# Attention probabilities split in SBUF and transposed by DMA instead of on TensorE

## The reference

```python
q = (x @ Wq).reshape(B, N, HEADS, DIM_HEAD).transpose(0, 2, 1, 3)   # 128 x 16 heads x 32 x 64
k = (context @ Wk).reshape(...)                                     # context: 257 rows of 96 for each sequence
v = (context @ Wv).reshape(...)
attn = softmax(einsum('bhnd,bhmd->bhnm', q, k) * SCALE)
out = einsum('bhnm,bhmd->bhnd', attn, v)
return out.transpose(0, 2, 1, 3).reshape(B, N, HEADS * DIM_HEAD) @ Wo + bo
```

## Time and profile before

| | before |
|---|---|
| median of the runs shown | 1027.83 us (1026.02 to 1030.45, 3 runs) |
| the profiled execution, its time | 1028.92 us |
| its span in the profile | 1027.0 us |
| TensorE busy | 870.6 us, 85% |
| VectorE busy | 831.1 us, 81% |
| GpSimd busy | 774.3 us, 75% |
| ScalarE busy | 684.0 us, 67% |

### The profile page before, as it was taken

One profiled execution on the slowest core, in us unless ns is written; L12 is line 12 of the kernel. 1 busy time (PEld: TensorE's weight loads), 2 busy tenths in 40 slices (PEclk: granted clock), 3 DMA queues, 4 the chain that ended last, 5 costly groups with the idle time before them and its releaser, 6 DMA issues.

```text
span 1027.0 us, 29818 instructions
## 1 busy us (share of the span) xinstructions
PE 870.6 (85%) x8554; PEld 720.6 (70%) x8554; DVE 831.1 (81%) x2343; ACT 684.0 (67%) x2029; POOL 774.3 (75%) x1237
## 2 busy tenths in 40 slices
PE   7989998999999999999999999999998461049895
PEld 7777786878787887878787887887776261036664
DVE  5899888989999989899999999998988657025563
ACT  3777776778777778778777777777775113037774
POOL 5788888898989898888889898989886503735554
PEclk9999999999999999999999999999999655559998
DMA  9111111111111111111111211111100840111120
GB/s 233 33 33 33 32 33 33 33 33 36 49 42 32 31 31 31 31 31 31 31 31 32 59 33 31 31 31 31 31 2 2 129 162 14 52 43 53 47 54 17
DMA packets 56836, 45.11 MB, mean 44 GB/s; under 512 B 8367, under 2 KB 54578, under 8 KB 56769
## 3 DMA queue, kind: packets, MB, share of 16 engines
q1 hardware_dynamic: 54464, 40.01, 15.9%
q0 software_dynamic: 2304, 4.25, 1.3%
HBM read 37.25 MB, written 7.52 MB: 44 GB/s over the span
## 4 chain that ended last, share of the span: by engine, by line
PE 36%; POOL 31%; issue 13%; DVE 12%; ACT 4%; DMA 1%; POOLq 1%; DVEq 1%; ACTq 0%; SPq 0%
POOL Pn L925 10%; PE bank L396 6%; PE bank L373 6%; PE bank L420 4%; POOL cT L916 4%; PE bank L1369 3%; PE bank L413 3%; PE bank L385 3%; POOL sorted_rows L1232 3%; POOL chi L906 2%; PE bank L1384 2%; DVE cs L839 2%; DVE nmax L783 2%; POOL clo L910 2%; DVE Tl L777 1%
## 5 line engine op out<-in xcount | busy, mean ns | idle before, releaser
L925 POOL TENSOR_TENSOR Pn<-Pe,rsum 128x1028 f32<-128x1028 f32 x128 | 243.1, 1899 | 74.4 <-DVE rsum L798 74.4
L713 ACT ACTIVATE Pe<-bank,nmax 128x257 f32<-128x257 f32 x512 | 240.5, 475 | 30.1 <-DVE nmax L783 29.5
L783 DVE TENSOR_REDUCE nmax<-bank 128x1 f32<-128x257 f32 x512 | 202.0, 415 | 35.3 <-PE bank L373 34.0
L373 PE MATMUL bank<-cT,qh 96*128 96x257 f16 x1024 | 184.8, 275 | 21.1 <-ACT Pe L713 19.6
L777 DVE TENSOR_TENSOR Tl<-bank,Th 128x512 f16<-128x512 f32 x256 | 173.8, 680 | 0.5 <-ACT Th L702 0.4
L702 ACT ACTIVATE Th<-bank 128x512 f16<-128x512 f32 x256 | 141.3, 595 | 48.5 <-PE bank L420 48.5
L420 PE MATMUL bank<-identf,Pn 128*128 128x128 f32 x1024 | 149.3, 274 | 0.0
L373 PE MATMUL bank<-cT,ql 96*128 96x257 f16 x512 | 139.2, 272 | 0.0
L420 PEld LDWEIGHTS bank<-identf,Pn 128*128 128x128 f32 x1024 | 115.1, 142 | 6.1
L373 PEld LDWEIGHTS bank<-cT,qh 96*128 96x128 f16 x1024 | 90.3, 97 | 38.3 <-issue 15.9
L713 ACT ACTIVATION_READ_ACCUMULATOR Pe<-bank,nmax 128x1 f32 x512 | 103.8, 203 | 0.0
(11 more groups left out here) (213 smaller groups left out, 2444.4 us busy)
## 6 DMA issues: line engine op xcount, KB each, us to landing
rawT<-in_dram SPq DMA_DIRECT2D x32, 385.5 KB, 3.9
raw<-in_dram SPq DMA_DIRECT2D x32, 384.0 KB, 4.4
sorted_rows<-fill SPq DMA_DIRECT2D x1, 2620.0 KB, 21.1
xs<-sorted_rows SPq DMA_DIRECT2D x40, 65.5 KB, 1.8
R<-in_dram SPq DMA_DIRECT2D x4, 512.0 KB, 5.9
Z<-last_rows SPq DMA_DIRECT2D x128, 2.2 KB
w1r<-in_dram SPq DMA_DIRECT2D x4, 512.0 KB, 13.7
w2fr<-in_dram SPq DMA_DIRECT2D x4, 512.0 KB, 14.2
```

What stands on the lines that cost most here:

```text
L373: last = nc.tensor.matmul(bank[SB[t]][:, 0:M], w[:, par, b, t * P:(t + 1) * P], cT[:, s4, c, 0:M], start=(k == 0), stop=(k == 2))
L713: nc.scalar.activation(Pe[:, n_par(j + 1), t, :], bank[SB[t]][:, 0:M], ACT.Exp, bias=nmax[:, n_par(j + 1), t:t + 1], accum_out=sums[:, n_p ...
L783: nc.vector.tensor_reduce(nmax[:, n_par(j + 1), t:t + 1], bank[SB[t]][:, 0:M], AX.X, ALU.max, negate=True).then_inc(s_nmax, 1)
L925: nc.gpsimd.tensor_tensor(Pn[:, par, :, :], Pe[:, par, :, :], rsum[:, par, :].unsqueeze(2).broadcast_to([P, QT, M]), ALU.mult)\
```

## The change

The probabilities are no longer transposed before they are split. ScalarE writes the high halves of Pn itself and VectorE the low halves, both into one SBUF tensor PHL, in two pieces h of two tiles each. A piece is 128 x 1024 f16, laid out as high or low (2), tile (2), column (256). SP then issues one crossbar DMA transpose for each piece into PT, which TensorE reads in `pe_pv`. The transposes of L420 are gone, as are Th and Tl. SP now follows the same steps as the other engines, and its context and Z loads stand between the transposes.

```diff
@@ pe_pv
-        def pe_pv(n, par, s8, gp, b, pairs):
+        def pe_pv(n, par, s8, gp, b, pairs, turns):
             wait(nc.tensor, s_Ol, n)
             k = 0
-            for w, p, s in ((chi, Th, s_Th), (clo, Th, None), (chi, Tl, s_Tl)):
+            for h in range(2):
+                wait(nc.tensor, s_T[par][h], 16 * turns)
+            for w, hl in ((chi, 0), (clo, 0), (chi, 1)):
                 for c in range(MC):
-                    if s is not None:
-                        wait(nc.tensor, s, MC * n + c + 1)
-                    nc.tensor.matmul(bank[6][0:CC, :], w[:, s8, c, :], p[:, par, c, :], start=(k == 0), stop=False)
+                    p = PT[:, par, :, :, :].rearrange("p h (l t c) r -> p h l t c r", l=2, t=2)
+                    nc.tensor.matmul(bank[6][0:CC, :], w[:, s8, c, :], p[:, :, hl, :, c, :], start=(k == 0), stop=False)
                     k += 1
@@ pe_step
-                wait(nc.tensor, s_pn, n + 1)
-                pe_probsT(n, n_par(j), 0)
             pe_mix(it, j, n)
             pe_early(n)
-            if exists(n):
-                pe_probsT(n, n_par(j), 1)
@@ act_step
-            if exists(n - 1):
-                wait(nc.scalar, s_PV, n - 2)
-                for c in range(MC):
-                    wait(nc.scalar, s_T, MC * (n - 1) + c + 1)
-                    nc.scalar.activation(Th[:, n_par(j - 1), c, :], bank[4 + c][:, :], ACT.Copy).then_inc(s_Th, 1)
+            if exists(n):
+                for h in range(2):
+                    wait(nc.scalar, s_T[n_par(j)][h], 16 * (4 * it + j // 2))
+                wait(nc.scalar, s_pn, n + 1)
+                for h in range(2):
+                    nc.scalar.activation(PHL[:, n_par(j), h, 0, :, :], Pn[:, n_par(j), 2 * h:2 * h + 2, 0:MC * P], ACT.Copy)\
+                        .then_inc(s_Ph, 1)
@@ dve_step
-                if kind == "low" and exists(n - 1):
-                    wait(nc.vector, s_Th, MC * (n - 1) + t + 1)
-                    nc.vector.tensor_tensor(Tl[:, n_par(j - 1), t, :], bank[4 + t][:, :], Th[:, n_par(j - 1), t, :],
-                                            ALU.subtract).then_inc(s_Tl, 1)
+                if kind == "low" and exists(n):
+                    wait(nc.vector, s_Ph, 2 * n + t + 1)
+                    nc.vector.tensor_tensor(PHL[:, n_par(j), t, 1, :, :], Pn[:, n_par(j), 2 * t:2 * t + 2, 0:MC * P],
+                                            PHL[:, n_par(j), t, 0, :, :], ALU.subtract).then_inc(s_Pl, 1)
@@ pool_step
-                wait(nc.gpsimd, s_T, MC * n)
+                wait(nc.gpsimd, s_Pl, 2 * n)
@@ SP
-            with sp.Fori(1, G // 2) as i:
-                for par in range(NP2):
-                    load_ctx(2 * i + par, par)
-                    load_z(2 * i + par, par)
+            def sp_step(it, j):
+                n, g, jj, gp = where(it, j)
+                if exists(n):
+                    wait(sp, s_PV, n - 1)
+                    for h in range(2):
+                        wait(sp, s_Pl, 2 * n + h + 1)
+                        sp.sem_inc(s_go)
+                        sp.dma_start(PT[:, n_par(j), h, :, :], PHL[:, n_par(j), h, :, :, :], transpose=True)\
+                            .then_inc(s_T[n_par(j)][h], 16)
+                if jj == 0 and exists(g + 2, G) and (n_static(n) is None or g >= 0):
+                    load_ctx(g + 2, gp)
+                if jj == 1 and exists(g + 1, G) and (n_static(n) is None or g >= 1):
+                    load_z(g + 1, 1 - gp)
+            pipeline(sp, sp_step)
```

More of the change, by code:

```diff
@@ L202, in perceiver_layer_kernel @@
         s_L12 = sem("s_L12")
-        s_T = sem("s_T")
-        s_Th = sem("s_Th")
-        s_Tl = sem("s_Tl")
+        s_T = [[sem(f"s_T{par}{h}") for h in range(2)] for par in range(NP2)]
+        s_go = sem("s_go")
+        s_Ph = sem("s_Ph")
+        s_Pl = sem("s_Pl")
         s_PV = sem("s_PV")
@@ L273, in perceiver_layer_kernel @@
         e12p = asb("e12p", [P, NP2, P], F16)
-        Th = asb("Th", [P, NP2, MC, Q], F16)
-        Tl = asb("Tl", [P, NP2, MC, Q], F16)
+        PHL = asb("PHL", [P, NP2, 2, 2, 2, MC * P], F16)
+        PT = asb("PT", [P, NP2, 2, 2 * 2 * MC, P], F16)
         L12 = asb("L12", [P, NP2, P], F16)
@@ L415, in pe_y @@
             last.then_inc(s_y, 1)
[L417 to L422, removed]
         def n_static(n):
@@ L442, in pe_step @@
                 pe_pv(n - 1, (j - 1) % NP2, (j - 1) % NC8, ((j - 1) // GB) % NP2, (j - 1) % GB,
-                      it + 1 + (j - 1) // NC8)
+                      it + 1 + (j - 1) // NC8, 4 * it + (j - 1) // 2 + 1)
             if exists(n - 5):
```

## The result

The changed kernel takes 1187.15 us in the median (1184.99 to 1192.66), the kernel before on the same chip 1026.92 (1025.72 to 1030.45): a ratio of 1.156, interval 1.151 to 1.161. It is 160 us slower. The profiled execution took 1186.75 us.

The account below looks back on a forecast made before the run. TensorE and VectorE lay close to the trip's length, GpSimd fixing some intervals; the change adds a ring and port waits. Steady trips 625, first four 232, last intervals 45: 902 against 759.5, +142, so 1170 us; own range 1128 to 1200.

Parts of the forecast that it names:

- the ring: Loop: Pn, its split, next exponentials, reciprocal of their sums, next Pn; one pass, 6.14 us, bounds every step from below.
- the port: VectorE instructions with two SBUF inputs and GpSimd's lock each other out; trip 56.8 us, or 54.0 if they never wait.
- TensorE's relief: Eight f32 transposes a step leave TensorE, 0.88 us a step, 7.0 a trip; priced at nothing.
- Rival 2: Loop: TensorE was the pace and ScalarE never waits for Pn; faster, 981 us; chance 0.05.
- the sum: Whole attention loop: eleven steady trips 625, first four 232, last seven intervals 45, together 902 us against 759.5.
- my loop without the port: Attention loop if subtractions never meet GpSimd: trips of 54.0 us, 858 us in all, execution 1128.
- The two SBUF inputs: Low-half subtractions beside GpSimd's chi, clo, cT: VectorE 0.2 us late, GpSimd 0.8, paid in its two full intervals.
- The single intervals: Eight step intervals of a steady trip, from j = -1 to 0 onward, each priced; together 56.8 us.
- The first four trips: Start of the loop, two trips without later-stage work, 20 us for setup work on VectorE; 232 us.
- Rival 3: Loop: TensorE's clock falls; a tenth of the steps at the lower level adds 40 us, 1210; chance 0.06.
- Rival 1: DMA transposes pace the loop beyond about 3.4 us each; 1270 us at 3.9, 1830 at 6.1; chance 0.25.
- the mark of rival 3: Sign that TensorE's clock had fallen: a granted clock under 0.95 in the loop.

Follow-up runs that it names:

- experiment 1: Kernel before, with one added wait: ScalarE may not begin step n until Pn of n is there; 1116.38 us, ratio 1.087.
- experiment 4: Changed kernel, low halves' second input read from a PSUM bank of zeros, subtraction of the high half left out; 1132.11 us, ratio 1.101.
- Experiment 2: Changed kernel, with the eight f32 transposes a step put back on TensorE into banks nobody reads; 1186.5 us, ratio 1.155.
- experiment 11: Kernel before, with two f32 transposes a step on TensorE instead of eight, zeros in the other tiles' columns; 1045.77 us, ratio 1.013.
- experiment 3: Changed kernel, every DMA transpose issued twice, the second into another tensor PT2, PV waiting for both; 1279.93 us, ratio 1.247.
- experiment 6: Changed kernel, split moved between qh and the last exponential, low halves behind ql; 1160.51 us, ratio 1.129.
- versions 5 and 10: Changed kernel; 5: split behind exponentials of tiles 0 and 1, 1200.27 us; 10: also low halves behind maxima, Z loads spread, zeros in PSUM, 1085.41 us.

## Why the prediction was right, point by point

**The mechanism and its size.** Forecast 1170 us, measured 1187, inside the forecast's own range of 1128 to 1200. The loss is the ring first and the port second, as put, and both were shown alone (experiments 1 and 4).

**TensorE's relief at nothing.** Right, and shown twice (2, and 11 in its two trips at full clock). Rival 2, that TensorE was the pace, is out.

**The ring of 6.14 us.** Measured 6.19. The only leg off by more than 0.05 is the split, 1.06 for 0.95. As a term of the sum the ring was priced too high: my loop without the port was 858 us, experiment 1 gives 845.6. The intervals into j = 3 and 4 were put at 6.8 each, where it shows 6.67 and 6.66, and the one into j = -1 at 7.75, where it shows 7.03. Some 17 us more of the loop (862.6 in experiment 4) belong to the DMA version beyond the ring. The split's slower pair and TensorE's clock (0.93 in the loop of experiment 4, 0.99 in that of experiment 1) are both candidates, and I have not told them apart.

**The two SBUF inputs.** Right in kind, too small: 902 - 858 = 44 us in the sum, 56 in the loop of experiment 4. I followed each half against one instruction of GpSimd's and gave a delay of 0.2 us to VectorE and 0.8 to GpSimd, so 8.04 us into j = 1. In the eleven steady trips the interval is 8.13 six times and 9.16 or 9.17 five times. VectorE's timeline in one of the five, and GpSimd's:

```profile
503.98 2.65 DVE L770 TENSOR_TENSOR PHL<-Pn,PHL 128x512 f16<-128x512 f32 x1
```

```profile
503.74 0.67 POOL L909 TENSOR_TENSOR cT<-rawT,cT 96x257 f16<-96x257 f32 x1
504.37 0.72 POOL L977 TENSOR_TENSOR oT<-num,rec 128x256 f32<-128x256 f32 x1
505.05 1.04 POOL L983 TENSOR_TENSOR mdx<-dx,mix 128x512 f32<-128x512 f32 x1
```

The subtraction needs 0.68 us and got its turn after three of GpSimd's instructions. Then two maxima, the second half and ql come late, and the Pn at 509.38 waits 1.12 us for rsum.

What brings the two engines together there is TensorE's clock one interval earlier. That interval in the trip shown and in one with 8.13 (columns as in the earlier trace rows):

```profile
494.02:500.21 6.19, 3.91 (x28) 2.57 (x27) 4.49 (x11) 3.79 (x13) 5.25 (x7) 0.85 0.25 48
551.11:557.30 6.19, 3.91 (x45) 3.12 (x43) 4.50 (x11) 4.30 (x14) 5.26 (x7) 1.00 0.25 48
```

The granted clock in it is 0.85 or 0.86 in the five trips with the long interval, and 0.96 to 1.00 in the six others. TensorE idles for 2.28 us up to 497.60, then two products of PV take 1.06 us (498.41). ScalarE waits 1.65 us for a later product, starts the split at 503.31, 3.10 us after Pn's start instead of 1.93, and the low half falls on cT, oT and mdx instead of clo. Experiment 2 repeats the pair: 9.32 to 9.34 us in the three trips with 0.78 or 0.79, 8.08 to 8.10 in the eight with 1.00. In experiment 4, without the port, the clock falls to 0.77 to 0.87 in seven trips and the interval stays at 7.23 to 7.42. So it takes both, and the 56 us of that experiment hold these 5 x 1.04 us.

**The single intervals.** In the trip from 551.11: 6.19, 8.13, 6.19, 7.59, 7.15, 6.88, 7.12, 7.30, where the sum had 6.14, 8.04, 6.14, 7.0, 7.7, 6.9, 7.13, 7.75. It comes to 56.55 for 56.8; the mean of the eleven steady trips is 631.2 / 11 = 57.4, with the trips of 9.17. The fourth was too low by 0.6, the fifth and the last too high by about as much. So part of the agreement is errors that cancel. The first four trips took 238 us for 232, the last seven intervals 48.9 for 45.

**Rival 3, the clock.** It came in part: the granted clock is 0.91 in the trip from 551.11, under the 0.95 that I named. In that trip's third interval TensorE idles 3.22 us, then two products of PV take 1.06 us where two take 0.60 just before, and in the fourth interval VectorE's small copy waits 1.87 us for TensorE. TensorE's and VectorE's timelines:

```profile
569.02 0.40 PE L374 MATMUL bank<-cT,qh 96*128 96x257 f16 x2 [3.22 <-ACT Pe L706]
...
569.37 0.60 PE L398 MATMUL bank<-PT,chi 128*96 128x512 f16 x2
...
570.42 1.06 PE L398 MATMUL bank<-PT,chi 128*96 128x512 f16 x2
```

```profile
573.34 0.23 DVE L796 COPY L<-bank 128x128 f16<-128x128 f16 x1 [1.87 <-PE bank L447]
```

So the fourth interval is 7.59 and not 7.0. In the eleven steady trips it is 7.10 to 7.12 in the five with a granted clock of 1.00 in it, and 7.55 to 8.34 in the six with 0.80 to 0.97. My reason against this rival, that TensorE idles under 2 us at a time, was wrong. Beyond 7.11 the six lose 4.3 us together, and with the 5.2 of the intervals of 9.17 that is some 10 us for eleven trips, and not the 40 us that I gave it. (In that price TensorE's 5.1 us a step should have been 4.7, from its 38 us a trip.)

**Rival 1, the transposes as the pace.** Not in this kernel: PV waits 3.8 us in all. My price of 2.4 to 3.1 us each was too high for the packets. 324800 packets less the 54464 of the earlier trace rows are 270336, or 1056 a transpose. Their share of time, 45.0% of 16 x 1184.7 us less 15.9% of 16 x 1027, is 5917 us, 21.9 ns a packet and 1.44 us a transpose. But the margin was not where I had it: landing takes 3.2 us and an issue on SP 1.24, which I had left out. Twice as many transposes cost 93 us (experiment 3), and with the same ones issued later PV waits 112 us for them (experiment 6).

**Forecast marks that did not hold.** I wanted TensorE's busy share in the loop under 75%; it is 41.43 of 57.09 us in one trip (73%), 42.86 of 56.55 (76%) in the other, and 696.0 of 918.2 (76%) in the whole loop. At the lower clock the same products stay busy longer. Pn starts 7.17 us apart in the mean of the steady trips and 7.23 in the whole loop, where I had 6.9 to 7.1. And the mark of rival 3 was met: the granted clock is 0.90 in the loop, where the kernel before has 1.00.

## What to carry to other kernels

Before moving an operation to an earlier step of a software pipeline, list what its engine does behind it and see whether its input depends on that: if so, a ring is closed, and its legs, added up, bound every step, whatever work was saved. When an operand moves from PSUM to SBUF on VectorE, look at what GpSimd does in that place, and count on more than one of its instructions. Work taken off a busy engine gains nothing where another chain sets the step, and the granted clock of TensorE has to be looked at again: it fell in experiment 11 and in the changed kernel, and one late product was enough to bring VectorE and GpSimd together. When an operation is moved to open a ring, follow the chain through the other engines too: versions 5 and 10 closed another one.

## What the runs showed of the hardware beyond what was expected

- A VectorE instruction with two SBUF inputs can be held for 2.65 us instead of 0.68, over three GpSimd instructions in a row. Swapping one input to PSUM took 55 us off one kernel and 96 off another. Which instructions it meets hung on TensorE's clock: 8.13 us for the interval behind a granted clock of 0.96 or more, 9.17 behind 0.85.
- A crossbar transpose of 128 x 1024 f16 from SBUF to SBUF: 1.24 us of issue on SP, 3.2 us to landing, 1056 packets, 1.44 us on 16 engines. With twice as many, SP's issues (1.23 to 1.35 us, one of 2.70) and the loads fill 26 of 30.9 us, and the 16 engines are at 0.81.
- Fewer transposes on TensorE made the kernel before slower by 1.3%, and the step into j = 0 took 5.04 us at a granted clock of 1.00 and 5.22 to 6.30 at 0.50 to 0.71. What lowers the clock was not tried.
